# A Strassen product taken over all four blocks of input channels instead of two, in a pyramid-pooling attention kernel

## The reference

```python
qk = relu(bn(conv1x1(x, qk_w)))             # 256 channels
val = relu(bn(conv1x1(x, v_w)))             # 512 channels
key = psp(qk)                               # max pooling to 1+9+36+64 = 110 cells
value = psp(val).transpose(0, 2, 1)
query = qk.reshape(B, Ck, H * W).transpose(0, 2, 1)
scores = softmax(query @ key * Ck ** (-0.5))
y = scores @ value
return x + bn(conv1x1(y, out_w))
```

## Time and profile before

| what | value |
|---|---|
| median of 3 runs | 1375.12 us (1374.86 to 1377.72) |
| profiled execution | 1374.09 us, span 1372.3 us, clock 0.999 |
| TensorE | 1341.9 us busy, 5786 matmuls |
| VectorE, ScalarE, GpSimd busy | 967.1, 633.3, 755.5 us |
| DMA | 213.46 MB, 156 GB/s |

### The profile page before, as it was taken

The page is one execution under the profiler, slowest core; times in us unless marked ns, Lnnn a source line. Parts: engine busy times, 40 slices in busy tenths (PEclk is TensorE's granted clock), DMA queues, the critical chain, the costliest instruction groups (busy, mean ns, idle before and its releaser), DMA issues.

```text
span 1372.3 us, 17075 instructions
## 1 busy us (share of the span) xinstructions
PE 1341.9 (98%) x5786; PEld 1077.6 (79%) x5786; DVE 967.1 (70%) x2262; ACT 633.3 (46%) x991; POOL 755.5 (55%) x469
## 2 busy tenths in 40 slices
PE   7999899999999999999999999999999998999997
PEld 6777678888888888878888878888788877888875
DVE  6555776677776687776776777676876678886566
ACT  4333455443545444545344545444455445664422
POOL 2655656555665546665456665556655535774522
PEclk9999999999999999999999999999999999999999
DMA  5211134445544435544345543535534435997326
GB/s 200 92 62 62 62 105 142 153 136 171 184 141 139 151 123 184 184 143 138 118 154 184 184 139 95 186 133 185 184 124 142 159 130 190 311 313 246 133 92 245
DMA packets 110344, 213.46 MB, mean 156 GB/s; under 512 B 6538, under 2 KB 6578, under 8 KB 110258
## 3 DMA queue, kind: packets, MB, share of 16 engines
q1 hardware_dynamic: 109682, 211.33, 46.4%
q10 hardware_dynamic: 576, 1.05, 0.2%
HBM read 145.25 MB, written 67.11 MB: 155 GB/s over the span
## 4 chain that ended last, share of the span: by engine, by line
PE 88%; DVE 3%; ACT 1%; issue 1%; DVEq 0%; ACTq 0%
PE conv_ps L570 20%; PE conv_ps L572 19%; PE conv_ps L571 19%; PE out_ps L661 4%; PE out_ps L662 4%; PE out_ps L663 4%; PE conv_ps L559 3%; PE conv_ps L557 3%; PE conv_ps L558 3%; PE score_ps L634 2%; PE score_ps L633 2%; PE score_ps L632 2%; PE sum_ps L644 1%; PE sum_ps L645 1%; PE sum_ps L672 0%
## 5 line engine op out<-in xcount | busy, mean ns | idle before, releaser
L1163 DVE TENSOR_REDUCE row_max<-conv_ps 128x64 f32<-128x384 f32 (+2 forms) x576 | 285.5, 528 | 196.1 <-ACT q L904 91.2
L449 POOL TENSOR_TENSOR xl<-xa,xh 128x512 fp32r<-128x512 f32 x162 | 267.7, 1672 | 254.0 <-ACT xh L844 254.0
L570 PE MATMUL conv_ps<-xh,wh 128*128 128x512 f32 x891 | 350.2, 393 | 2.4 <-DVE conv_ps L1229 2.2
L572 PE MATMUL conv_ps<-xl,wh 128*128 128x512 f32 x891 | 349.5, 392 | 0.0
L571 PE MATMUL conv_ps<-xh,wl 128*128 128x512 f32 x891 | 347.8, 390 | 0.0
L479 POOL TENSOR_TENSOR q_l<-q,q_h 128x1024 fp32r<-128x1024 f32 x64 | 154.1, 2408 | 175.6 <-ACT q_h L910 175.6
L570 PEld LDWEIGHTS conv_ps<-xh,wh 128*128 128x128 f32 x891 | 167.7, 188 | 41.1 <-DVE conv_ps L1229 5.4
L572 PEld LDWEIGHTS conv_ps<-xl,wh 128*128 128x128 f32 x891 | 167.6, 188 | 37.1
L571 PEld LDWEIGHTS conv_ps<-xh,wl 128*128 128x128 f32 x891 | 167.6, 188 | 36.2
L844 ACT ACTIVATE xh<-xa 128x512 fp32r<-128x512 f32 x162 | 124.6, 771 | 68.0 <-PE conv_ps L572 68.0
L1304 DVE TENSOR_TENSOR xo<-out_ps,xo 128x512 f32<-128x512 f32 x226 | 148.1, 681 | 1.6 <-PE out_ps L663 0.7
(11 more groups left out here) (218 smaller groups left out, 2289.2 us busy)
## 6 DMA issues: line engine op xcount, KB each, us to landing
xa<-x SPq DMA_DIRECT2D x148, 512.0 KB, 4.7
xo<-x SPq DMA_DIRECT2D x115, 512.0 KB, 4.6
out<-xo SPq DMA_DIRECT2D x115, 512.0 KB, 3.1
q<-x SPq DMA_DIRECT2D x8, 512.0 KB, 4.7
out<-q SPq DMA_DIRECT2D x8, 512.0 KB, 3.3
q<-v_w ACTq DMA_DIRECT2D x4, 256.0 KB, 4.5
q<-out_w SPq DMA_DIRECT2D x1, 1024.0 KB, 7.9
out<-xa SPq DMA_DIRECT2D x2, 512.0 KB, 3.4
```

Source lines behind the costliest of these rows:

```text
L449: nc.gpsimd.tensor_tensor(xl[:, b0:b1, :], raw, xh[:, b0:b1, :], ALU.subtract).then_inc(x_lo, 1)
L570: nc.tensor.matmul(out[:, :], hi, xh[:, b, :], start=start, stop=False, skip_group_check=True)
L572: return nc.tensor.matmul(out[:, :], hi, xl[:, b, :], start=False, stop=stop, skip_group_check=True)
L1163: last = nc.vector.tensor_reduce(row_max[:, c, n, :], src[:, r0_ * W:r1_ * W].rearrange("p (r w) -> p w r", w=W), AX.X, ALU.max)
```

## The change

- The 7 multiplications of a product each cover two blocks of input channels, so that all four are inside Strassen's scheme; `plain` is gone. A product is 14 x 3 matmuls where it was 15 x 3.
- The operands xh and xl have 14 places, the sums T1 to T4 are 128x1024 each and have three places in tt, and each of the now 7 parts is 128x1024. The combinations of weights sh, sl are twice as wide.
- Room is made for that: the queries go to DRAM (`spill`, 256 KB each, four per step) and come back one tile at a time (`load_q`, 512 KB, two per step), both on SyncE's queue; the ring of residuals has 2 places instead of 3 for most tiles.
- The shift of the output is no longer added to the projected values (`make_values`, shift_bc, the four transposes at line 540); it is added with the residual, in one scalar_tensor_tensor. ScalarE's copy in the last stage adds it as bias.
- `finish_grids` uses four tensor_reduce in place of three tensor_tensor and one tensor_reduce. Keys and values are finished mostly on ScalarE. In batch-ending steps `finish_grids` for the keys and `refine` come ahead of `make_u4(s, 0)`.
- The fills are dealt out anew, so that each product has attention between its multiplications: u4 and u7 are each waited for after 6 matmuls and a fill, in an ordinary step.
- U7 is itself one of the four outputs, and is pooled when VectorE has made it.

```diff
-        OPS = 9
+        OPS = 7
...
-    q = sb("q", [P, NT, QC, TN])
+    q_out = sb("q_out", [P, 3, TN])
+    q_in = sb("q_in", [P, QC, TN])
...
-    nc.tensor.matmul(out[:, :], hi, xh[:, b, :], start=start, stop=False, skip_group_check=True)
...
+    for k in range(HALF):
+        first, end = start and k == 0, stop and k == HALF - 1
+        nc.tensor.matmul(out[:, :], hi[:, k, :], xh[:, b + k, :], start=first, ...)
+        nc.tensor.matmul(out[:, :], lo[:, k, :], xh[:, b + k, :], start=False, ...)
+        last = nc.tensor.matmul(out[:, :], hi[:, k, :], xl[:, b + k, :], start=False, stop=end, ...)
...
     times(u1, wh[:, K1, m1], wl[:, K1, m1], 0, start=True).then_inc(p1_done, 1)
     fill1()
-    pe.wait_ge(rows_pooled, g)
+    pe.wait_ge(rows_pooled, g if n == 0 else g - 2)
     times(u7, sh[:, 0, :, ms], sl[:, 0, :, ms], 8, start=True).then_inc(p5_done, 1)
     pe.wait_ge(u1_copied, n + 1)
     times(u6, sh[:, 1, :, ms], sl[:, 1, :, ms], 10).then_inc(u2_done, 1)
-    times(u1, wh[:, 1, m1], wl[:, 1, m1], 1)
-    plain(u1, m1, 4, stop=True).then_inc(conv_done, 1)
+    times(u1, wh[:, K2, m1], wl[:, K2, m1], 4, stop=True).then_inc(u1_done, 1)
     fill2()
     pe.wait_ge(u4_made, n + 1)
     times(u6, sh[:, 2, :, ms], sl[:, 2, :, ms], 2).then_inc(u3_done, 1)
-    times(u5_bank, sh[:, 3, ms], sl[:, 3, ms], 3)
-    plain(u5_bank, m1, 6, stop=True).then_inc(conv_done, 1)
+    times(u5_bank, sh[:, 3, :, ms], sl[:, 3, :, ms], 6, stop=True).then_inc(u5_done, 1)
     fill3()
     pe.wait_ge(u7_made, n + 1)
-    plain(u6, m2, 4, stop=False).then_inc(x0_used, 1)
-    times(u6, wh[:, 1, m2], wl[:, 1, m2], 10, stop=True).then_inc(conv_done, 1)
-    plain(u7, m2, 6, stop=True).then_inc(conv_done, 1)
+    times(u6, wh[:, K2, m2], wl[:, K2, m2], 12, stop=True).then_inc(u6_done, 1)
     fill4()
```

SyncE's list in a step, and GpSimd's at the start:

```diff
+    sp.wait_ge(x_lo, x_parts(s) + 4)
+    sp.wait_ge(t_made, 4 * s)
     load(2 * s + 2)
+    spill(s - 1, 3); store(2 * A - 4)
+    sp.wait_ge(x_lo, x_parts(s) + 6)
     load(2 * s + 3)
+    load_residual(2 * A - 2); store(2 * A - 3); load_q(A + 1)
+    load_residual(2 * A - 1); store(2 * A - 2); load_q(A + 2)
+    load_residual(2 * A); store(2 * A - 1); load_residual(2 * A + 1)
+    spill(s, 0); spill(s, 1); spill(s, 2)
...
-    first_sums(1)
-    split_parts_lo(1)
+    split_part_lo(1, 0); split_part_lo(1, 3)
+    make_t1(1); split_part_lo(1, 1); make_t2(1); split_part_lo(1, 2)
+    make_t3(1); split_part_lo(1, 4); split_part_lo(1, 5)
+    make_t4(1); split_part_lo(1, 6)
```

VectorE:

```diff
-    grid_chain(nc.vector.tensor_tensor(g6, part6[:, cs, 0::2, :], part6[:, cs, 1::2, :], ALU.max))
+    grid_chain(nc.vector.tensor_reduce(g6, part6[:, cs, :, :].rearrange("p c (r n) w -> p c r w n", n=2), AX.X, ALU.max))
...
-    nc.vector.tensor_tensor(xt, out_bank(a, m)[:, :], xt, ALU.add).then_inc(out_added, 1)
+    nc.vector.scalar_tensor_tensor(xt, out_bank(a, m)[:, :], shift[:, CC + m:CC + m + 1], xt, ALU.add, ALU.add)
```

More of the change, by code:

```diff
@@ L392, in _ @@
                     load(s + 2)
+                if s == LAST:
+                    spill(PAIRS - 1, 3)
+                    store(FOUR - 2)
+                if s - NT + 1 < LAST:
+                    load_q(s - NT + 1)
                 ap = s - NT - 1
@@ L770, in _ @@
                     conv(s, 4)
[L771 removed]
+                    conv(s, 5)
                 project(ap, 0)
@@ L912, in exps, with finish_values @@
+            def finish_values(k):
+                act.wait_ge(values_pooled, k + 1)
+                for m in range(VC):
+                    last = nc.scalar.activation(cells[:, m, :], cells[:, m, :], ACT.Relu, bias=shift[:, m:m + 1])
+                last.then_inc(value_step, 1)
+                act.wait_ge(value_step, k + 1)
+                nc.scalar.activation(value_h[:, :, 0:CELLS], cells[:, 0:VC, :], ACT.Copy).then_inc(value_hi, 1)
             def exps(a):
@@ L1050, in copy_out @@
                 wait(act, y_added, a - LAST - 1)
-                nc.scalar.activation(copy_of(a), out_bank(a, COPIED)[:, :], ACT.Copy).then_inc(y_copied, 1)
-            for m in range(OC):
-                last_values_hi(m)
+                nc.scalar.activation(copy_of(a), out_bank(a, COPIED)[:, :], ACT.Identity,
+                                     bias=shift[:, CC + COPIED:CC + COPIED + 1]).then_inc(y_copied, 1)
+            values_hi(B - 1)
             exps(S - 1)
@@ new lines, in finish_grids @@
+                grid_chain(nc.vector.tensor_reduce(rows3[:, cs, :, :], g6.rearrange("p c (r n) w -> p c r w n", n=2),
+                                                   AX.X, ALU.max))
+                grid_chain(nc.vector.tensor_reduce(g3, rows3[:, cs, :, :].rearrange("p c r (w n) -> p c r w n", n=2),
+                                                   AX.X, ALU.max))
+                last = nc.vector.tensor_reduce(cells[:, cs, CELL1:CELL3], cells[:, cs, CELL3:CELL6], AX.X, ALU.max)
+                if done is None:
+                    grid_chain(last)
+                else:
+                    last.then_inc(done, 1)
@@ L1257, in finish_keys, with keys_lo, cell_values_lo @@
+            def keys_lo(k):
+                dve.wait_ge(key_hi, k + 1)
                 nc.vector.tensor_tensor(key_l[:, :, 0:CELLS], key_d[:, :, :], key_h[:, :, 0:CELLS], ALU.subtract)\
                     .then_inc(key_ready, 1)
-            n_values = [0]
-            def finish_values(c0, c1):
-                cs = slice(c0, c1)
-                if c0 == 0:
-                    wait(dve, vo_lo, n_values[0])
-                    n_values[0] += 1
-                for m in range(c0, c1):
-                    last = nc.vector.tensor_scalar(value[:, m, :], cells[:, m, :], shift[:, m:m + 1], 0.0, ALU.add, ALU.max)
-                grid_chain(last)
-                grid_chain(nc.vector.tensor_copy(value_h[:, cs, 0:CELLS], value[:, cs, :]))
-                nc.vector.tensor_tensor(value_l[:, cs, 0:CELLS], value[:, cs, :], value_h[:, cs, 0:CELLS], ALU.subtract)\
+            def cell_values_lo(k):
+                dve.wait_ge(value_hi, k + 1)
+                nc.vector.tensor_tensor(value_l[:, :, 0:CELLS], cells[:, 0:VC, :], value_h[:, :, 0:CELLS], ALU.subtract)\
+                    .then_inc(value_ready, 1)
@@ L1273, in finish_values, with finish_last_values @@
+            def finish_last_values(m):
+                grid_chain(nc.vector.tensor_scalar(cells[:, m, :], cells[:, m, :], shift[:, m:m + 1], 0.0, ALU.add, ALU.max))
+                grid_chain(nc.vector.tensor_copy(value_h[:, m, 0:CELLS], cells[:, m, :]))
+                nc.vector.tensor_tensor(value_l[:, m, 0:CELLS], cells[:, m, :], value_h[:, m, 0:CELLS], ALU.subtract)\
                     .then_inc(value_ready, 1)
@@ L1463, in _ @@
                     add_out(ap, 3)
+                    split_e_lo(ac)
+                    values_lo(ac // NT)
                     continue
                 if s == LAST + 1:
-                    values_lo(ap // NT)
+                    pool_tile_rows(s, 5)
+                    refine(ap)
+                    normalise(ap)
                 split_e_lo(ac)
```

714 lines of the change are left out of this document (398 added, 316 removed).

## The result

| | before | after |
|---|---|---|
| median | 1375.12 us (5 runs, four of 1373.65 to 1377.72 and one of 1518.32) | 1383.91 us (5 runs, 1382.48 to 1389.10) |
| ratio | | 1.0072, 95% interval 1.0045 to 1.0098 |
| profiled execution, span, clock | 1374.09, 1372.3, 0.999 | 1382.48, 1380.7, 0.978 |
| TensorE, VectorE, ScalarE, GpSimd busy | 1341.9, 967.1, 633.3, 755.5 | 1303.5, 949.1, 687.8, 951.6 us |
| DMA | 213.46 MB, 156 GB/s | 272.20 MB, 197 GB/s |

A forecast was written before the change was run, and what follows sets the result against it. TensorE was taken to bound the steps. Matmuls saved 55.9 us; with the other engines' losses and gains the terms summed to -37.9, taking the profiled 1374.1 to 1336.2 and the median to 1337 us, range 1318 to 1356.

The forecast's parts named there:

- DMA: Spills and loads of queries add 57 MB; loads of x and residuals land in time; booked at 0.
- In the last image: Last image: grids' tensor_tensor no longer on VectorE's list and make_values goes; -2.0 us, bounds -5 and +4.
- Rival 3: Loads of x come late, held on SyncE's list; 4.0 us per step over 23 steps, 1424 us; chance 5%.
- The matmuls: All products: 243 matmuls fewer at 0.230 us, -55.9 us, 2.07 per step; an ordinary step takes 38.2 us.
- Inside a product: make_u4 and make_u7 fit behind fewer matmuls; +0.2 us per step over 23 attention steps, +4.6.
- Step 1: GpSimd's last low part ends at 62.6, needed at 57.3: +5.3 us, plus +2.0 for the clock; bounds 2 and 10.
- Steps 2 and 3: Steps 2, 3 and 4 each start 2.0 us late, waiting for GpSimd's last part; +6.0 in all.
- The grids: Step 4: reductions with one input avoid the delay beside GpSimd, TensorE's wait and the fallen clock; -4.1 us.
- Batch-ending steps: Five steps, 8 to 24: make_u4 of j = 0 1.0 us late, make_u7 of j = 2 0.9 late; +9.5.

The follow-up runs named there:

- a1: Changed kernel without the seven loads of queries from DRAM in the last image's key tiles (that output left out): 1350.29 us.
- a4: Changed kernel with a second place for returning queries in the last stage, each load issued a tile earlier: 1350.84 us, ratio 0.984.
- c3: Changed kernel plus two query places, step 1's last high part later, and in batch-ending steps add_out(B0, 2) later, split_p_hi(A) earlier: 1335.56 us, ratio 0.9718.
- d2: c3 with the first key tile's conv(s, 5) and ScalarE's copy of it put back where the kernel before has them: 1332.11 us, ratio 0.9689.
- b5: Kernel before with three matmuls fewer per product and nothing else, part of the result missing: 1336.08 us.
- b1: Changed kernel with ScalarE's high part of step 1's last sum moved behind its copies of U1 and P5: 1381.57 us.
- b4: Kernel before with the grids' three two-input maxima as one-input reductions: 1370.69 us, ratio 0.9967.
- b3: Changed kernel with the three grid reductions as two-input tensor_tensor again: 1419.07 us.
- b2: Changed kernel with make_u4(s, 0) ahead of the keys' grids and refine in batch-ending steps: 1388.02 us.

## Why the prediction was wrong

**The failed step** is the end of "DMA", *booked at 0*, with "In the last image ... **-2.0**, bounds -5 and +4". I followed the loads of x and the residuals through the ordinary step and did not follow the loads of queries through the last image at all. There the tiles come every 10 us instead of two in 38, and the place for queries is one. The runs showed instead a round of 17.3 us through that one place, which set the pace of the tiles and made the stage 42.5 us longer where -3.9 was booked from step 27 on. From rows that I had, the round could be added up: three operations of GpSimd at 2.41, a landing of 6.2, a high part at 1.06, 14.5 us before any queueing, against a tile of 10. a1 and a4 show this to be worth 35 of the stage's 42.5 us; c3 to d2 show 3.3 more to be the order at the first key tile, which the diff changed and I didn't mention; 4.0 stay unexplained, so what came of the booked -2.0 can't be said.

**Rival 3**, loads on SyncE's list in order, held by a wait for another engine, was near to the right mechanism, in the wrong place: I priced it for x in the 23 attention steps, where it doesn't occur (ordinary steps have no wait of TensorE), gave it 5%, and never asked the same of each other load in each stage.

**The matmuls** are right: 3402 of them on the product's lines (three times 648 and 486), an ordinary step at 38.27 us. b5 adds that this doesn't come by itself: in the kernel before a third of the time of the matmuls that go (0.72 of 2.07 us per step) is lost again, most of it to a new wait. **Inside a product** the booked +0.2 per step was 0.1 at most (38.27 against 38.2). VectorE was never late in an ordinary step, though its additions took 746 ns each, not the 0.70 booked.

**Step 1** was mis-sized: 5.3 + 2.0 booked at the last low part, 10.00 measured, and from 52 us on, not from 57; behind it 13 matmuls came 0.43 apart, 2.6 us; start to step 2 came out 4.9 worse than booked. GpSimd's list was nearly right (its last low part ends at 64.0, my table had 62.6). My table was wrong in ScalarE's list: I did not see that `copy_u1(1, 0)` is behind the last sum's high part. b1 shows it: the wait falls to 2.81 + 3.42.

**Steps 2 and 3** waited 1.3 us each for GpSimd, where 2.0 was booked; step 4 waited 0.66 for it, and 1.8 us for VectorE, which wasn't booked there. **The grids** (-4.1) measured 3.5 to 3.8 (b4), and b3 shows what the reductions also spared in the changed kernel, 35 us: I had this rule beside the term and did not price it for five batch-ending steps with a busier GpSimd. What I had said against the change is there too: `keys_lo`, which keeps two SBUF inputs, took 1.49 to 2.13 us in the five batch-ending steps beside GpSimd and 0.38 in step 4, where GpSimd was idle. In step 8 it stood ahead of the addition that waited for its residual anyway, so no cost of it is shown there. **Batch-ending steps** lost more than 1.9, in another way. Such a step now has 183 matmuls (and the step behind it 161 where others have 166), which is 42.1 us at 0.230; it took 45.0 on average, so 2.9 were lost: U4 of j = 0 was late as forecast (0.49, booked 1.0), U7 of j = 2 wasn't; the others were a residual's landing, which I had in time by 1.3 us and which VectorE waited 3.26 for, and p's low part in front of the scores. Removing these two brought such a step from 45.0 to 43.5.

**The sum of the steps** hid these errors, since 34.1 came where 34.0 was booked: +4.9, -1.8 and -3.2 cancel. That is luck, not a sign that the terms were right. c3 comes out at 1335.56, where 1337 was forecast, but with edits that the forecast didn't have, so that it doesn't bear the forecast out; d2 is 42 us below the kernel before on its chip.

## What to carry to other kernels

When data moves from a resident buffer to DRAM and back, add up one whole round of its place (last reader, the queue up to the issue, the landing, the first reader) and hold it against the shortest period in any stage, not against the ordinary step's; if the round is longer, a second place was the remedy here (34.8 us), and another order on the one queue gave 14.1 of them. When one instruction is moved, move what every other engine does with its result, or it will stand in the old place and hold up what follows it. Where the engine named by a wait had waited itself, go on to the next list until something is found that stands for no engine's work: here a free place and a queue.

## What the runs showed of the hardware

- The DMA moved 337 and 344 GB/s at a share of 0.96 and 0.97 in a stretch of 34 us (a4, d2) in which TensorE was busy for all of it; in the changed kernel it waited at 217 GB/s, so not for bytes. The landing of 512 KB was 5.5 us (x) and 4.2 us (queries, residuals) in the median, and 6.95 from the issue to the first reader in the round above.
- In b3 a VectorE operation of 128x18 with two SBUF inputs took 2.25 us beside GpSimd's 2.34 and ended with it, and 0.18 where GpSimd was idle; the one-input reduction right behind it took 0.17 in both places.
- `scalar_tensor_tensor` with a PSUM input, a per-partition scalar and an SBUF input took 746 ns at 128x512, where the `tensor_tensor` that it replaced took 681 ns.
- After the waits of 3.8 to 10.0 us in the changed kernel the next matmuls lasted 0.63 us and came 0.43 apart, at the clock's lower level, 1.2 GHz; after the waits of 0.5 to 0.7 us in steps 2 and 3 they came 0.23 apart. In 1150 to 1184 the mean granted clock was 0.80. The length of the wait alone doesn't tell what it costs: 8 matmul starts were 0.43 apart behind a wait of only 1.90 us (1105.55, after) and none behind one of 2.36 (810.18, b2); behind the same wait of 4.40 us in the last stage there were 7 in a4 and 12 in c3.
